# Feed-forward rows split into f16 parts before the turn, and turned by DMA a tile ahead

## The reference

```python
x = x + xattn(layernorm(x), ctx_2048, ctx_2048, wq, wk, wv, wo)
x = x + attn(layernorm(x), W_Q, b_Q, W_K, b_K, W_V, b_V, W_O, b_O)
x = x + ffn(layernorm(x), gate_up_packed, gate_up_scales, down_packed, down_scales)

def ffn(x):                              # hidden size 1408
    gate_up = x @ w_gu.T                 # w_gu: fp4 value * scale per group of 128 inputs
    gate, up = gate_up[..., :1408], gate_up[..., 1408:]
    y = (silu(gate) * up) @ w_down.T
    return y / sqrt(mean(y * y) + 1e-6)
```

## Time and profile before

| | us |
|---|---|
| median of three runs | 1349.93 (1348.22 to 1350.03) |
| profiled execution, span from first to last instruction | 1349.0 |
| TensorE busy | 1327.4 |
| VectorE busy | 1019.0 |
| ScalarE busy | 514.4 |
| GpSimd busy | 384.2 |

### The profile page before, as it was taken

One profiled execution on the slowest core, in us unless ns is written; L12 is line 12 of the kernel. 1 busy time (PEld: TensorE's weight loads), 2 busy tenths in 40 slices (PEclk: granted clock), 3 DMA queues, 4 the chain that ended last, 5 costly groups with the idle time before them and its releaser, 6 DMA issues. The chain is left out here.

```text
span 1349.0 us, 23490 instructions
## 1 busy us (share of the span) xinstructions
PE 1327.4 (98%) x9232; PEld 773.9 (57%) x9232; DVE 1019.0 (76%) x2336; ACT 514.4 (38%) x1268; POOL 384.2 (28%) x304
## 2 busy tenths in 40 slices
PE   8999999999999999999999999999999999999998
PEld 6666666646666666666666666654444434444443
DVE  7444444269988888887888878858999798689594
ACT  4333333253333334343343334320001476666661
POOL 0000000012333222332223322313043296757571
PEclk9999999999999999999999999999999999999999
DMA  9555544541100220012210124155661000000002
GB/s 344 211 207 204 203 188 188 219 179 48 33 21 28 64 64 32 17 32 63 64 32 17 32 64 156 38 140 170 147 234 63 1 1 1 1 0 7 26 1 94
DMA packets 41766, 122.57 MB, mean 91 GB/s; under 512 B 4280, under 2 KB 6968, under 8 KB 34232
## 3 DMA queue, kind: packets, MB, share of 16 engines
q1 hardware_dynamic: 40488, 118.19, 25.8%
q10 hardware_dynamic: 1168, 2.88, 1.0%
HBM read 95.89 MB, written 25.17 MB: 90 GB/s over the span
## 5 line engine op out<-in xcount | busy, mean ns | idle before, releaser
L191 PE MATMUL psum<-xt_hi,hqk_hi 128*128 128x512 f16 x512 | 194.4, 380 | 0.0
L192 PE MATMUL psum<-xt_lo,hqk_hi 128*128 128x512 f16 x512 | 194.0, 379 | 0.0
L193 PE MATMUL psum<-xt_hi,hqk_lo 128*128 128x512 f16 x512 | 194.0, 379 | 0.0
L919 POOL TENSOR_TENSOR hd_rotated<-hd_products 64x512 f32<-64x512 f32 x32 | 40.8, 1274 | 419.7 <-DVE hd_products L1181 419.7
L1576 POOL TENSOR_TENSOR ff_part<-ff_part 128x512 f32<-128x512 f32 x88 | 129.1, 1470 | 79.9 <-DVE ff_part L1708 79.4
L1708 DVE SCALAR_TENSOR_TENSOR ff_part<-psum,gu_scale,ff_part 128x512 f32<-128x512 f32 x176 | 122.6, 743 | 33.1 <-PE psum L1602 28.3
L193 PE MATMUL psum<-hd_wv_hi,xt_lo 128*128 128x256 f16 x512 | 139.6, 273 | 0.0
L192 PE MATMUL psum<-hd_wv_lo,xt_hi 128*128 128x256 f16 x512 | 139.6, 273 | 0.0
L191 PE MATMUL psum<-hd_wv_hi,xt_hi 128*128 128x256 f16 x512 | 139.6, 273 | 0.0
L1601 PE MATMUL psum<-xt_hi,gu 128*128 128x512 f16 x352 | 133.7, 380 | 3.3 <-DVE ff_part L1708 2.7
L1602 PE MATMUL psum<-xt_lo,gu 128*128 128x512 f16 x352 | 133.4, 379 | 0.0
(11 more groups left out here) (202 smaller groups left out, 3094.0 us busy)
## 6 DMA issues: line engine op xcount, KB each, us to landing
xa_kv_t<-in_ctx_t_dram SPq DMA_DIRECT2D x16, 1024.0 KB, 5.4
xa_kv<-in_ctx_dram SPq DMA_DIRECT2D x16, 1024.0 KB, 4.9
w_rows<-in_head_weights_dram SPq DMA_DIRECT2D x10, 1024.0 KB, 8.5
z_scratch<-hd_z_hi SPq DMA_DIRECT2D x32, 256.0 KB, 2.6
z_scratch<-hd_z_lo SPq DMA_DIRECT2D x32, 256.0 KB, 3.3
hqk_lo<-z_scratch SPq DMA_DIRECT2D x8, 1024.0 KB, 7.5
w_rows<-z_scratch SPq DMA_DIRECT2D x8, 1024.0 KB, 8.0
xn<-in_x_dram SPq DMA_DIRECT2D x8, 512.0 KB, 4.1
```

The lines of the kernel that those rows point to most:

```text
L191: pe.matmul(out, lh, rh, start=(first and i == 0), stop=False)
L192: pe.matmul(out, lh, rl, start=False, stop=False)
L193: last = pe.matmul(out, ll, rh, start=False, stop=(final and i == k - 1))
```

## The change

The turn of the feed-forward's rows no longer goes through TensorE and PSUM. ScalarE rounds a row block of `xn` to f16 (`xn_hi`), GpSimd subtracts (`xn_lo`), and SyncE issues two DMAs with transpose for each row block, one per part, 128 rows of 512 numbers each, straight into `xt_hi` and `xt_lo`: eight DMAs a tile. There are two pairs of turned buffers, for even and odd tiles, so that a tile is turned while the one before is multiplied. For tile 0 this is done in the merge: SyncE between the second-half load for tile 1 and the first-half load for tile 2, GpSimd behind its eighth bias addition, ScalarE between its two loads of codes, after it has waited for all stores of z. For tiles 1 to 3 ScalarE and GpSimd do a row block each at the start of the hidden block `block_after(t, i)` (3, 5, 7, 9 in tile 0; 5, 6, 7, 8 in tiles 1 and 2). TensorE's sixteen transposes a tile and their evacuations by ScalarE and VectorE are gone, as are the turned units in the order of PSUM banks. Some buffers move: `gate` and `hidden` into the free end of `hqk_lo`, `xn_hi` and `xn_lo` of the feed-forward into the free ends of `wo_hi` and `wo_lo`.

```diff
+        xn_hi, xn_lo = sb("xn_hi", [P, TT, D], F16), sb("xn_lo", [P, TT, D], F16)
+        xn_hi_done, xn_lo_done = sem("xn_hi_done"), sem("xn_lo_done")
...
                 sp.wait_ge(z_used[1], t)
                 load_z(t, 1)
+                if t == 1:
+                    for i in range(TT):
+                        sp.wait_ge(xn_lo_done, i + 1)
+                        for by_row, to in ((xn_hi, xt_hi), (xn_lo, xt_lo)):
+                            sp.dma_start_transpose(to[:, :, i * P:(i + 1) * P], by_row[:, i, :]).then_inc(xt_turned[0], 16)
...
                 pool.tensor_tensor(x2[b // TT][:, b % TT, :], x2[b // TT][:, b % TT, :], early.b_o, ALU.add).then_inc(x1_ready, 1)
+                if b == 2 * TT - 1:
+                    for i in range(TT):
+                        pool.wait_ge(xn_hi_done, i + 1)
+                        pool.tensor_tensor(xn_lo[:, i, :], xn[:, i, :], xn_hi[:, i, :], ALU.subtract).then_inc(xn_lo_done, 1)
...
             for g in range(2, KD):
                 act.wait_ge(gu_decoded, g - 1)
                 act.dma_start(codes[g % 2], codes_of(gu_codes, g)).then_inc(gu_loaded[g % 2], 16)
+                if g == 2:
+                    act.wait_ge(z_stored, 16 * (HEADS_SMALL + 2 * NT * PAIRS))
+                    for i in range(TT):
+                        act.wait_ge(xn_ready, i + 1)
+                        act.activation(xn_hi[:, i, :], xn[:, i, :], ACT.Copy).then_inc(xn_hi_done, 1)
...
-        gate = sb("gate", [P, 2, TILE], F32)
-        hidden = sb("hidden", [P, 2, TILE], F32)
+        xts = ((xt_hi, xt_lo), (sb("odd_xt_hi", [P, KD, TILE], F16), sb("odd_xt_lo", [P, KD, TILE], F16)))
...
-        tile_0 = [("x", 0, k) for k in range(KD)] + [("p", 0, u, g) for u in range(UNITS) for g in range(KD)]
-        in_order = []
-        for t in range(1, NT):
-            in_order += [("x", t, k) for k in range(KD)] + [("p", t, u, g) for u in range(UNITS) for g in range(KD)]
+        tile_0 = [("p", 0, u, g) for u in range(UNITS) for g in range(KD)]
+        in_order = [("p", t, u, g) for t in range(1, NT) for u in range(UNITS) for g in range(KD)]
...
+        def unit_scaled(t, i):
+
+            return 4 * (i + 1) if t == 0 else 8 + 2 * i
+
+        def block_after(t, i):
+
+            return unit_scaled(t, i) // 2 + 1
...
+            def turn_xn(t):
+
+                if t >= 2:
+                    banks.wait_filled(sp, None, ("p", t - 2, UNITS - 1, KD - 1))
+                for i in range(TT):
+                    sp.wait_ge(xn_lo_done, (t - 1) * TT + i + 1)
+                    for by_row, to in zip((xn_hi, xn_lo), xts[t % 2]):
+                        sp.dma_start_transpose(to[:, :, i * P:(i + 1) * P], by_row[:, i, :]).then_inc(xt_turned[t % 2], 16)
+
+            for t in range(1, NT):
+                turn_xn(t)
...
+                    for i in range(TT):
+                        if t < NT - 1 and b == block_after(t, i):
+                            n = t * TT + i
+                            pool.wait_ge(xn_hi_done, n + 1)
+                            pool.tensor_tensor(xn_lo[:, i, :], xn[:, i, :], xn_hi[:, i, :], ALU.subtract).then_inc(xn_lo_done, 1)
...
-            def turn_xn(t):
-                if t:
-                    pe.wait_ge(xn_ready, t * TT)
-                for k in range(KD):
-                    unit = ("x", t, k)
-                    banks.wait_room(pe, None, unit)
-                    for i in range(TT):
-                        last = pe.transpose(psum_of(unit)[:, block_of(i)], xn[:, i, block_of(k)], ident[:, :])
-                    banks.fills(last, None, unit)
-
             def gate_up(t, u, g):
                 first = u % 2 * FF + u // 2 * P
                 unit = ("p", t, u, g)
-                if u == 0:
-                    banks.wait_moved(pe, None, ("x", t, g))
+                xt_hi, xt_lo = xts[t % 2]
+                if u == 0 and g == 0:
+                    pe.wait_ge(xt_turned[t % 2], 32 * TT * (t // 2 + 1))
...
-            turn_xn(0)
             for u in range(UNITS):
                 for g in range(KD):
                     gate_up(0, u, g)
             for t in range(NT - 1):
-                for i, b in jobs[0:FIRST]:
-                    down(t, i, b)
-                turn_xn(t + 1)
-                for i, b in jobs[FIRST:SECOND]:
+                for i, b in jobs[0:SECOND]:
                     down(t, i, b)
                 for u in range(UNITS):
...
-            def first_halves(t):
-                for k in range(KD):
-                    banks.wait_filled(act, None, ("x", t, k))
-                    act.activation(xt_hi[:, k, :], psum_of(("x", t, k)), ACT.Copy).then_inc(xt_hi_done, 1)
+            def first_half(t, i):
+                if t and i == 0:
+                    act.wait_ge(xt_turned[t % 2], 32 * TT * (t // 2 + 1))
+                act.wait_ge(xn_ready, t * TT + i + 1)
+                act.activation(xn_hi[:, i, :], xn[:, i, :], ACT.Copy).then_inc(xn_hi_done, 1)
...
-            first_halves(0)
             for t in range(NT):
                 for b in range(FB + 2):
+                    for i in range(TT):
+                        if t < NT - 1 and b == block_after(t, i):
+                            first_half(t, i)
                     if b < FB:
...
-                    if b == FB and t < NT - 1:
-                        first_halves(t + 1)
...
-            def second_halves(t):
-                for k in range(KD):
-                    unit = ("x", t, k)
-                    dve.wait_ge(xt_hi_done, t * KD + k + 1)
-                    banks.moves(dve.tensor_tensor(xt_lo[:, k, :], psum_of(unit), xt_hi[:, k, :], ALU.subtract), None, unit)
-
...
-                if i == 0:
-                    for k in range(KD):
-                        banks.wait_filled(dve, None, ("x", t - 1, k))
+                if i == 0 and t >= 2:
+                    dve.wait_ge(xn_lo_done, (t - 1) * TT)
...
                 if t == 0:
-                    if u in (4, 8, 12, 16):
-                        scale_block(1, u // 4 - 1)
+                    for i in range(TT):
+                        if u == unit_scaled(0, i):
+                            scale_block(1, i)
                     return
                 if t < NT - 1:
                     if u in (0, 2, 4, 6):
                         statistics(t + 1, (u // 2 + 1,))
-                    if u in (8, 10, 12, 14):
-                        scale_block(t + 1, u // 2 - 4)
+                    for i in range(TT):
+                        if u == unit_scaled(t, i):
+                            scale_block(t + 1, i)
                 if t >= 2:
                     if u == 11:
...
-            second_halves(0)
...
-                    if b == FB and t < NT - 1:
-                        second_halves(t + 1)
...
+        xt_turned = [ctx.enter_context(nc.semaphore(f"xt{n}_turned")) for n in range(2)]
...
+        spare = flat[:, 2 * FB * TILE:].bitcast(F32)
+        gate, hidden = (spare[:, i * 2 * TILE:(i + 1) * 2 * TILE].rearrange("p (n t) -> p n t", n=2) for i in range(2))
+        xn_hi, xn_lo = (w[:, :, :].rearrange("p a n -> p (a n)")[:, FB * TILE:FB * TILE + TT * D].rearrange("p (b d) -> p b d", d=D) for w in (wo_hi, wo_lo))
```

12 lines of the change are left out of this document (6 added, 6 removed).

## The result

The changed kernel takes 1367.62 us (median of 4 runs, 1365.02 to 1369.32) against 1349.7 us for the kernel before beside it: 1.0136 times as long, 95% interval 1.0124 to 1.0148. The forecast was slower, 1357.0 us; the loss is 17.9 us where I had 7.1. The profiled execution spans 1367.5 us.

What follows compares the result with a forecast made beforehand. TensorE, busy 98% of the span, bounds tiles 1 to 3 but not tile 0. Merge +8.0, clock +1.6, tile 0 +1.0, removed turns -3.5 sum to +7.1 us: 1357.0 us, own range 1353 to 1362, overall 1346 to 1369.

Steps and rivals of the forecast that it cites:

- Part 1: Start of feed-forward tile 0: without its transposes, VectorE's first scaling comes sooner, -2.3 us for what follows.
- Part 2: Tiles 2 and 3: removed TensorE transposes save 2 x 1.75 = 3.5 us; GpSimd's added subtractions cost nothing.
- Part 3: Tile 0: four subtractions lengthen GpSimd's full line, its h_lo delays the last down products; +1.0 us, bounds -4.1 and +4.
- Rival C: z is late, but GpSimd does not bind tile 0: -4.1 in place of +1.0, 1351.9 us; chance 0.15.
- Part 4: Merge: z loads issued later, sharing DMA engines with the later codes load, so TensorE waits for z; +8.0 us, bounds -0.6, +21.
- rival A: Merge: crossbar transfers are slow and z queues behind them; at 30 us for eight, +20 us, 1370 us; chance 0.12.
- Rival B: Merge: z lands in time because codes are nearly done; -2.5 to -5 us, 1346 us; chance 0.15.
- Part 5: Behind the merge's stop TensorE runs partly at 1.2 GHz instead of 2.4; +1.6 us, 0 to 3.2.
- Part 6: Merge: subtractions and later codes delay VectorE, covered by its waits; nothing, or up to 3 us without parts 4 and 5.
- Part 7: Crossbar transfers of later tiles land in time: 8 us for the last two, enough at 3.7 us each; no cost.
- signs of being wrong: Wrong if z is issued before 962 or lands before 980, or if tile 0 ends 4 us sooner.

Runs made afterwards that it cites:

- kernel 1: The changed kernel, but in the merge SyncE issues the z loads for tile 2 ahead of the eight transposing transfers; 1352.95 us.
- Kernel 11: Kernel 6 with VectorE's steps for the square root moved from units 11 and 13 to units 1 and 3; 1349.04 us.
- Kernel 8: Kernel 1 with only GpSimd's four subtractions in tile 0 left out; 1346.12 us.
- kernel 3: The changed kernel, with ScalarE waiting for the eight merge transfers to land before it issues the last codes load; 1370.65 us.
- kernel 4: The changed kernel with the eight merge transfers as plain copies, same bytes and 256-byte runs, no transpose; 1363.83 us.
- kernel 7: Kernel 1 with all of GpSimd's twelve subtractions in the feed-forward (for tiles 1 to 3) left out; 1344.22 us.
- kernel 9: Kernel 1 with tile 1 turned by TensorE as in the kernel before, so no GpSimd subtractions in tile 0; 1349.87 us.
- kernel 2: The changed kernel, but ScalarE issues its last codes load before it makes xn_hi in the merge; 1357.64 us.
- kernel 10: Kernel 1 with VectorE's steps for the square root moved from units 11 and 13 to units 1 and 3; 1347.72 us.
- kernel 6: The changed kernel, with the eight merge transfers issued after SyncE's loads of the down weights; 1349.62 us.

## Why the prediction was right in sign and wrong in size

The sign was right, and the order of the terms: the merge costs most, tile 0 eats its own gain, the removed turns don't make up for it. Point by point:

**Part 1, the start (-2.3): right.** From the merge's last product to VectorE's first scaling: 5.3 us before (1066.17 in the earlier trace rows), 2.9 now (1078.88), -2.4.

**Part 2, the turns of tiles 2 and 3 (-3.5): the gain is real, "Nothing" for GpSimd was wrong.** From tile 1 to the end the changed kernel needs +0.8, so 4.3 us were lost again (233.9 us; kernel 1, whose profile has the same two stops and no slow products, needs 232.2). Kernel 11, with the root moved, needs 230.05 us (1115.35 to 1345.4) against 233.1: -3.0, with a stop of 0.64 us left. That is the -3.5. The failing step is the sentence that GpSimd gets four subtractions "where it is busy 35.6 us of 50": I read a share of busy time, and not who runs beside it. The trace before had the pattern in a row I quoted for another part: VectorE's 0.34 us step taking 1.29, "one step an add". The very chain of tile 2 has it in the trace before, at 1217.46 and 1218.61. I priced it in the merge and not here.

**Part 3, tile 0 (+1.0): right in a trace without slow products, by another way.** The cycle grew by 0.88 us (forecast 0.8). GpSimd's h_lo of block 8 ends 54.0 us after the feed-forward's first product (1131.36 less 1077.38) against 52.8 before, +1.2. In kernel 1, tile 0 takes 54.79 us against 53.62 (1062.29 in the earlier trace rows to 1115.91), +1.2. But TensorE doesn't wait for h_lo. It waits earlier, for a PSUM bank, through ScalarE, 2.69 us in one piece, and in the changed kernel's profile seven slow products follow: +2.6 in all. The forecast had the bound and not the place, and so no clock term here. Kernel 8 gives the price without subtractions: 50.9 us, 3.9 less. Rival C is out.

**Part 4, the merge (+8.0): the mis-sized term, +12.9.** The stop is 13.53 us instead of 0.58. The codes load moved by 9.2 us (forecast 9.7) and GpSimd's subtractions were done at 967.5 (forecast 966.7). But z came out only at 982.80, when the codes were through: its lateness is the wait behind the transfers, and not the shared engines that the sum had. The step that failed is "these transfers spread over the engines like z; up to some 13 us for all eight, nothing changes". From first issue to z's issue they took 20.5 us. Alone they are fast: 1.3 us of issue each, 2.5 us to land, near the plain bytes, as kernel 3 shows. Beside the codes load they starve (kernel 3), transposing or not (kernel 4), and keep SyncE at the issue; that their small packets are the reason is argued. I also took the codes' packets for 1.4 KB, from rows of the load before; the one that the transfers met has 11 KB. I had let z share with the codes and had let the transfers share with nobody, though they started within a microsecond of them. This is rival A's chain (slow transfers, z queued behind, from 13 us on) at two thirds of its size, with a cause it didn't name; its 1370 us was nearer than my 1357, and I gave it 0.12. Rival B's condition came true only when z was moved ahead (kernel 1).

**Part 5, the clock behind the stop (+1.6): +2.8.** Fourteen products take 5.8 us instead of 14 x 0.216 = 3.0, most of the way to the upper bound of 3.2. Then 12.9 + 2.8 less 0.6, by which TensorE was ready earlier in this execution (976.98 against 977.61), make the 15.1 us.

**Part 6, VectorE in the merge (nothing): right where TensorE is late, and nearly used up without it.** VectorE waited 12.7 us for down scales in the changed kernel with no one behind it. In kernels 7 and 9, without the stop, the phase's end waits 3.1 and 2.2 us instead of 1.05: within the "up to 3 us". Kernel 3 went over the edge.

**Part 7, later transfers (in time): right.** They land in 2.4 to 3.3 us and no one waits.

Of my signs of being wrong none came true: z was not issued before 962, and tile 0 did not end 4 us sooner. I had set them only against a forecast too high.

In the spans, then, the forecast missed the merge by 5.5 us (15.1 against 9.6), tile 0 by 1.6 (2.6 against 1.0) and the rest by 4.3 (+0.8 against -3.5): 11.4 us together, which is 18.5 less 7.1. The medians miss by 10.8 (17.9 less 7.1).

## What to carry to other kernels

A transfer's price is its company and not only its bytes: before transfers with small packets go ahead of a load that TensorE needs, look which large-packet load another queue has running. Here the small ones waited for it and held the issuing engine. Put the load with the due date first and the transfers with slack last; here that order alone was worth 15 to 18 us. And work moved to GpSimd "where it has room" was paid by VectorE's small steps beside it, one GpSimd operation each: check what VectorE does in exactly those microseconds.

## What the runs showed of the hardware that I had not expected

- A transposing SBUF-to-SBUF transfer of 128 x 512 f16 takes 1.19 to 1.31 us of its issuing engine and lands in 2.4 to 3.3 us when no load runs; beside a load with 11 KB packets it lands up to 15.3 us after its issue and holds the engine up to 6.5 us. A plain copy with 256-byte runs is held as long (7.13 us; 0.65 when free), and in kernel 3 a pair of loads with rows of 2 KB was held 18.49 us.
- A VectorE step on four numbers a partition lasts 1.04 to 1.20 us instead of 0.16 when it begins beside a GpSimd operation on two tensors, and ends with it.
- Behind stops of 13.53, 11.15, 9.10 and 6.06 us TensorE began at half clock every time, for 14, 14, 9 and 7 products, and for 14 behind the 8.60 us at the end of the merge in kernel 3. Behind stops of 2.1 to 2.7 us the slow products came in some profiles (both times in the changed kernel and kernel 4, once each in kernels 2, 9 and 10) and not in others (kernels 1, 3, 6, 8 and 11), though kernels 1 and 10 have the same stop of 2.68 us; behind the 3.10 us of kernel 7 none came.
